# Attention on one Trainium2 core: which engine's guests stand in which PSUM bank, one down projection moved, unread products in two waits

## The reference

```python
x = x + attention_0(layernorm(x), ctx, W_k, b_k, ln_gamma, ln_beta)  # keys = values = ctx @ W_k.T + b_k
x = x + ffn_0(layernorm(x), w_gate, w_up, w_down)
x = x + attention_1(layernorm(x), ctx, ctx)                          # 32 query heads, 8 key-value heads of 16
x = x + moe(layernorm(x), gate_w, w0, w1, wo)                        # 8 experts, the best 2 of a token
```

```python
def h_bitlinear(x, w):
    return einsum('bsh,oh->bso', act_quant(fwht(x)), weight_quant(w))
y = h_bitlinear(silu(h_bitlinear(x, w_gate)) * h_bitlinear(x, w_up), w_down)
```

## Time and profile before

| | us |
|---|---|
| median of 3 runs | 1672.63 |
| lowest, highest | 1671.73, 1675.54 |
| span of the profiled execution | 1670.3 |

### The profile page before, as it was taken

The page is one execution under the profiler, slowest core; times in us unless marked ns, Lnnn a source line. Parts: engine busy times, 40 slices in busy tenths (PEclk is TensorE's granted clock), DMA queues, the critical chain, the costliest instruction groups (busy, mean ns, idle before and its releaser), DMA issues.

```text
span 1670.3 us, 24439 instructions
## 1 busy us (share of the span) xinstructions
PE 1567.2 (94%) x8124; PEld 1047.5 (63%) x8150; DVE 948.0 (57%) x1539; ACT 717.6 (43%) x1160; POOL 702.1 (42%) x479
## 2 busy tenths in 40 slices
PE   6869999999889999999899899999999999999998
PEld 4555657565543434434333778788788888788886
DVE  6998979796878897887885622222122222222221
ACT  5885646455547777777677211111111111111111
POOL 1124251633513125254354765670862180930064
PEclk9889999999898999999999999999999999999999
DMA  9189800000231445243430625231440140530088
GB/s 357 56 305 386 291 1 1 0 1 1 84 94 47 123 132 149 82 126 111 148 114 28 224 70 189 82 120 32 182 176 26 59 155 26 188 127 26 26 140 213
DMA packets 90944, 196.16 MB, mean 117 GB/s; under 512 B 7153, under 2 KB 9074, under 8 KB 90226
## 3 DMA queue, kind: packets, MB, share of 16 engines
q1 hardware_dynamic: 71746, 156.68, 28.2%
q0 software_dynamic: 7168, 17.04, 4.5%
q10 hardware_dynamic: 11952, 21.43, 3.9%
HBM read 113.28 MB, written 81.32 MB: 117 GB/s over the span
## 4 chain that ended last, share of the span: by engine, by line
PE 68%; DVE 16%; POOL 6%; ACT 4%; issue 3%; DMA 3%; another core or an unknown queue 0%; SPq 0%; POOLq 0%; DVEq 0%; ACTq 0%
PE psum L2929 11%; PE psum L2931 11%; PE psum L2930 11%; PE psum L2580 6%; DVE neg_max L2057 5%; PE psum L2782 5%; PE psum L2771 5%; PE psum L2744 4%; POOL expert_weight_parts L1052 3%; PE psum L2625 3%; PE psum L2595 2%; DMA w_of_even_expert<-in_L_ffn_w 2%; PE psum L2953 2%; POOL expert_weight_parts L1051 1%; DVE inner_rotated_t_second L1926 1%
## 5 line engine op out<-in xcount | busy, mean ns | idle before, releaser
L2057 DVE TENSOR_REDUCE neg_max<-psum 128x2 f32<-128x1024 f32 x248 | 291.3, 1220 | 49.5 <-PE psum L2744 48.3
L1420 ACT ACTIVATE probabilities<-psum 128x512 f32<-128x512 f32 x512 | 271.7, 601 | 85.2 <-PE psum L2771 81.3
L2199 DVE TENSOR_TENSOR expert_inner<-psum,expert_inner 128x512 f32<-128x512 f32 x78 | 53.9, 692 | 388.7 <-ACT expert_inner L1526 378.6
L2929 PE MATMUL psum<-expert_weight_parts,sorted_tokens_t_first 128*128 x624 | 250.8, 402 | 8.8 <-POOL expert_weight_parts L1052 5.1
L2930 PE MATMUL psum<-expert_weight_parts,sorted_tokens_t_first 128*128 x624 | 246.8, 396 | 0.0
L2931 PE MATMUL psum<-expert_weight_parts,sorted_tokens_t_second 128*128 x624 | 246.8, 395 | 0.0
L1526 ACT ACTIVATE expert_inner<-psum 128x512 f32<-128x512 f32 x78 | 46.7, 599 | 396.7 <-PE psum L2931 396.7
L2771 PE MATMUL psum<-query_rows,key_rows 50*128 50x512 f32 x512 | 179.3, 444 | 4.1 <-ACT probabilities L1420 3.0
L2744 PE MATMUL psum<-key_rows,query_rows 48*128 48x512 f32 x496 | 170.6, 491 | 11.7 <-DVE neg_max L2057 5.8
L2929 PEld LDWEIGHTS psum<-expert_weight_parts,sorted_tokens_t_first 128*128 128x128 f32 x624 | 117.7, 189 | 37.4 <-issue 11.1
L2782 PE MATMUL psum<-probabilities,value_and_one 128*32 128x512 f32 x1024 | 140.3, 620 | 0.8 <-ACT probabilities L1420 0.7
(11 more groups left out here) (316 smaller groups left out, 2924.3 us busy)
## 6 DMA issues: line engine op xcount, KB each, us to landing
sorted_x<-zero_rows SPq DMA_DIRECT2D x9, 3960.0 KB, 30.5
w_of_odd_expert<-in_L_ffn_w SPq DMA_DIRECT2D x8, 2048.0 KB
wo_of_expert<-in_L_ffn_wo SPq DMA_DIRECT2D x7, 2048.0 KB, 8.6
query_rows<-query_rows_of_units SPq DMA_DIRECT2D x64, 192.0 KB, 3.5
w_of_even_expert<-in_L_ffn_w SPq DMA_DIRECT2D x6, 2048.0 KB, 11.6
sorted_tokens<-sorted_x ACTq DMA_DIRECT2D x39, 264.0 KB, 2.8
sorted_y<-expert_out ACTq DMA_DIRECT2D x39, 256.0 KB
query_rows_of_units<-dims_first SPq DMA_DIRECT2D x32, 256.0 KB
```

The source lines that it names most:

```text
L1420: nc.scalar.activation(prob[t % 2][:, i * SEQ:(i + 1) * SEQ], bank[4 + n % 3], ACT.Exp, scale=HD ** -0.5).then_inc(c_e, 1)
L2057: nc.vector.tensor_reduce(of_pair[:, p, st, :], ring(("max", (m, i))).rearrange("p (h n) -> p h n", h=2), AX.X, ALU.max, negate=True).then ...
L2199: nc.vector.tensor_tensor(h, bank[2 * half + 1], h, ALU.mult).then_inc(e_h, 1)
L2929: nc.tensor.matmul(out_bank, hi[:, cols], w_r[:, bass.ds(w_at, 512)], start=start, stop=False)
```

## The change

- In phase C the jobs that ACT reads (`chunk`, `xt`, `logits`, `pick`, `rank`) leave the ring and take a bank of the scores' rotation over 4, 5 and 6, in ACT's own order. DVE's jobs keep the ring of two slots. `xt` is cut from two jobs of two token tiles (1024 columns) to four jobs of one (512 columns), in steps 1, 2, 3 and 3.
- From unit 30 on the scores rotate over five banks, 2 to 6, and DVE's few jobs over banks 0 and 1. The `attend` that stood between the third and the fourth score product there now comes behind the fourth.
- In the last batch of phase B, `down_projected(b - 1, 3)` leaves round 3 and stands behind the loop, its transposes in round 6 rather than 2, the copy of these, the update of x and the statistics accordingly. Behind it come three chunks, then `unread(16)`; the fourth chunk moves behind tile 1's rotation.
- `unread(24)` near the end of phase A, before `scales_spread(0)`; `unread(3)` behind each pair of maxima in unit -1.

```diff
@@ jobs and places
+        OF_VECTOR = ("router sums", "x dims")
+        jobs, jobs_at_end = [("negmax", 0)], []
...
+                of_ = jobs if there(u_ + 2) else jobs_at_end
...
+        place = {job: i % 2 for i, job in enumerate(jobs)}
+        place.update({job: 2 + i % 2 for i, job in enumerate(jobs_at_end)})
...
+        last_scores = scalar_jobs.index(("score", 16 * (UNITS - 2)))
+        scalar_place = {job: (4, 5, 6)[i % 3] for i, job in enumerate(scalar_jobs[:last_scores])}
+        scalar_place.update({job: (2, 3, 4, 5, 6)[i % 5] for i, job in enumerate(scalar_jobs[last_scores:])})
@@ ScalarE, phase B
                 silu_pair(b, 2)
-                if b:
+                if b and more:
                     inner_transposed(b - 1, 3)
...
+                else:
+                    inner_transposed(b - 1, 3)
                 silu_pair(b, PAIRS - 1)
@@ VectorE, phase B
-                    if b and r == 4:
+                    if b and more and r == 4:
                         tokens_updated(b - 1, 3)
...
                 second_part_of(b, 0, 1)
+                if not more:
+                    tokens_updated(b - 1, 3)
                 second_stage(b, 1)
...
+                if not more:
+                    tokens_statistics(b - 1, 3)
+                    queries_deviation(b - 1)
                 tokens_updated(b, 0)
@@ TensorE
                 weight_transposed(18)
+                unread(24, bank[4])
                 scales_spread(0)
...
-                    if b and r == 2:
+                    if b and r == (2 if more else 6):
                         inner_quantised_transposed(b - 1, 3)
-                    if b and r == 3:
+                    if b and more and r == 3:
                         down_projected(b - 1, 3)
...
-                    for chunk in (CTX_CHUNK, 0, 1, 2):
+                    down_projected(b - 1, 3)
+                    for chunk in (CTX_CHUNK, 0, 1):
                         chunk_transposed(0, chunk)
+                    pe.wait_ge(b_g, BATCH * FC)
+                    unread(16, bank[4])
...
                 if not more:
+                    chunk_transposed(0, 2)
                     chunk_transposed(0, 3)
...
+                of, at = (scalar_held, scalar_place[job]) if job in scalar_place else (held, place[job])
+                if at == 2 and of is held and held[2] is None:
+                    held[2] = held[3] = held[0]
+                if of is scalar_held and at == 2 and scalar_held[2] is None:
+                    scalar_held[2] = scalar_held[3] = held[1]
+                if of[at] is not None:
+                    pe.wait_ge(*of[at])
...
-                if n >= 3:
-                    pe.wait_ge(c_e, n - 2)
+                take(("score", n), c_e, n + 1)
...
-                                if p == 1 and h == 1 and not there(u + 2):
-                                    attend(ST * u + t - 1)
                                 score(u, t, p, h)
                             if there(u + 2):
                                 maximum(u + 2, 2 * t + p, 1 - h, h == 0)
+                        if u == -1:
+                            unread(3)
...
-            def batch_transposed(b, half):
-                pe.wait_ge(d_xn, b * ST + 2 * half + 2)
+            def batch_transposed(b, st):
+                pe.wait_ge(d_xn, b * ST + st + 1)
```

78 lines of the change are left out of this document (42 added, 36 removed).

## The result

The changed kernel takes 1661.8 us (median of 5 runs), the kernel before 1672.6 (5 runs): ratio 0.9934, 95% interval 0.9921 to 0.9947. The profiled execution of the changed kernel has a span of 1659.9 us, 10.4 less than before's 1670.3. My forecast was 1664.5.

A forecast was written before the change was run, and what follows sets the result against it. TensorE, busy 1567.2 of 1670.3 us, bounds the kernel; time lies in its idle, low clock or removable work. Terms 3.8 + 4.0 + 0.4 + 0.1 + 0.0 - 1.0 + 0.8 = 8.1 us gave 1662.2, plus 2.3: 1664.5 us; range 1657 to 1670.5.

The forecast's parts named there:

- The ternary gap: TensorE's idle stretch before the last batch's inner rotation: moving one down projection there and filling it saves 3.8 us.
- only about 0.3 survive: Inner rotation: of 2.6 us from a warm clock, about 0.3 us remain because VectorE is late next.
- The guests: ScalarE's jobs in attention's score banks: routing waits vanish, 1.0 us for each of three batches, 0.5 per rank, 4.0 us.
- My own steps (-0.83, +0.2, +0.3, -0.5): Routing in attention, one batch: first guest step 4.70 to 3.87 us, next +0.2, then +0.3, next unit's first step -0.5.
- The clock and the chunks: Mid attention: fewer stalls keep TensorE's clock up, 0.8 us; plain chunks in the score banks save at most 0.4 us.
- The start of attention: Unread products behind eight pairs of maxima cost 0.4 us and warm the clock: 0.1 us gained, ends -2.5 and +2.0.
- Phase A: 24 unread products before the products of the scales: 0.0 us, since TensorE waits for ScalarE anyway; ends -0.6 and +0.9.
- The last two units: End of attention: GpSimd's closed chain turns TensorE's gain into a longer VectorE wait: -1.0 us, ends -2.5 and 0.
- Rival A: End of attention: the last two units' gain carries through, +3.3 in place of -1.0, giving 1660.2 us; chance 0.12.
- D: Attention: guests take a score bank, so the next step's third product waits for their copy; slower, 1679.3 us; chance 0.07.
- C: Waits only change place: routing gives 1, the clock nothing, the ternary gap 3.45, the end -1: 1669.2 us; chance 0.15.
- B: Clock stays up at attention's start, the rotation's first tile and two of four falls: 1658.5 us; chance 0.10.

The follow-up runs named there:

- kind B: Label of chips, not a kernel: those of the first two groups of follow-up runs, where the kernel before took 1663.2 and 1663.7 us.
- the pair of kernels that differ there in nothing else: The kernel before with only ScalarE's guests moved into the score banks, ratio 0.9985, against the kernel before with the ternary part alone, ratio 0.9991.
- kind A: Label of chips, not a kernel: those of the first measurement and the last group of runs, where the kernel before took 1672.6 and 1673.6 us.
- the kernel with three banks: The changed kernel with the last two units as before the change (three score banks to the end): 1656.7 us, ratio 0.9961 to the kernel before.
- the last kernel: The changed kernel with batch 2's slots and row weights on VectorE and no unread products at all: 1659.6 us, ratio 0.9900 to the kernel before.

## Why the prediction was right, point by point

**The sum.** 8.1 us forecast, 10.4 measured. The terms were off both ways: the guests gave 2.7 more, clock and chunks 1.0 more, the last two units 0.8 more; the ternary gap and the start gave 0.5 less each, phase A with the loops behind it 0.35 less, and what comes behind the shift took 1.0. That they nearly cancel is luck, and so in part is the chip: on kind B the changed kernel gains 4.7 us (2.7 to 6.5), which 8.1 would have missed.

**The ternary gap**, 3.8 forecast, 3.3 measured. The 3.45 us of the loop came, the clock stayed up, and VectorE was late next, as worked out; the fill overran by 0.2 us instead of leaving 0.3. What failed is the step "only about 0.3 survive": nothing does, it is -0.1. Counted from the end of the loop, which was itself 0.35 late, the rotation starts 4.15 us earlier and not 3.45, because VectorE's steps ahead of it are less stretched (its first second stage takes 1.22 us for 2.17). Of that 3.8 are left at VectorE's `second_part_of` for tile 1, which comes 6.6 us behind TensorE's start and not 6.0, 3.6 at the quantising and 3.3 at the transposed maxima. I had costed the moved transposes and chunks at nothing; but GpSimd's split of the chunk behind the second tile now falls on VectorE's second stages (1.63 and 2.31 us for 1.21 and 1.22). Without the fill and with a cold start the stage is shorter: 24.66 to 24.67 us in four traces, 25.76 to 25.78 in all seven others of the place, six with the fill and one without it in which the clock stayed up. So what goes with the 1.1 us is whether the first tile runs cold, and that only the kernels without the fill did; that it then misses GpSimd's split is my reading. So the fill is not worth 0.3 us but costs up to 1.1. (Without the ternary part the stage takes 25.49, 25.45 and 24.67 us, the last with a shorter stretch at half clock: it is as sensitive there.) What I had said of the moved update of x held: 0.74 us beside GpSimd's subtraction, not stretched.

**The guests**, 4.0 forecast, 6.7 measured in these units, and 6.7 confirmed by the pair of kernels that differ there in nothing else. The mechanism was right and a term was mis-sized: a batch is worth 1.84, 1.85 and 1.5 us and not 1.0, a rank 0.75 and not 0.5. My own steps (-0.83, +0.2, +0.3, -0.5) add up to 0.83, which I wrote as 1.0. Step by step in units 12 and 13: 4.70 to 3.63 (I said 3.87), +0.16 (+0.2), +0.06 (I said +0.3), 4.60 to 3.93 (I said 0.5, it is 0.67), and the third step of unit 13, which I took as "small change", gave 0.33.

**The clock and the chunks**, 0.8 + 0.4 forecast, 2.2 between units 1 and 29 beside the routing units, 1.4 of it the fall at 628. That fall is in both traces of the kernel before and in one of the four traces of kind A with the guests; on kind B it is in no trace, without the guests either. So that the change took it away is not shown. The rest is not separable.

**The start of attention**, 0.1 forecast, -0.4 measured, within the ends. The pair with its unread products takes 1.30 us and not 1.18: I had added up the records and one start, not the step into and out of the full-row products twice per pair. The unread products did shorten the stretch at half clock: 3.4 to 13.7 us in the six traces with them, 13.7 to 23.9 in the eight without. But with them it begins at 504 to 507 us, behind the wait, and without them at 491 to 497, so that part of it passes ahead of that wait. Over all traces the start takes 34.9 to 38.4 us without the unread products and 35.6 to 39.6 with them. Warm products before a wait did not keep the clock up behind it.

**Phase A**, 0.0 forecast: nothing separable from the 0.35 us that the changed kernel lost by the start of batch 3's loop.

**The last two units**, -1.0 forecast, -0.2 measured. All of its parts but one are in the trace: the wait of 0.96 us for the last maxima (0.9 said), 2.9 us of lead that TensorE makes behind it (10.5 at unit 30, 13.4 at the last attended transposes), of which 2.1 are lost again in VectorE's wait of 2.99 us (3 us or more said) for GpSimd (0.91 before). The clock did fall over the last logits (in the changed kernel, line 2898 from 910.28 on):

```profile
909.20:912.50 3.30, 3.30 (x11) 0.75 (x10) 2.55 (x9) 0.86 (x2) 2.39 (x4) 0.50 0.78 291
```

But the 0.7 us for it did not reach the shift, which waits for GpSimd's reciprocal root. Rival A is excluded: kernels with three and with five banks end within 0.2 us.

**Rivals.** D, guests that take a score bank, is excluded by the units' lengths. C, the waits only change place, holds for the last two units alone; its total, 3.4 us, lies within what kind B shows, but not by its mechanism, for the units won 6.7 there too. B, the clock stays up, came true in the rotation, where it brought nothing, and at 628, and was false at the start and in unit 17.

**What stays open**: why a chip is of kind A or B, and with it why the gain over before is 0.66% on the one and 0.28% on the other (single traces put that difference between units 2 and 29: 8.9 us won there against 3.1); the 4 us total of the kernel with three banks; and the total of the last kernel.

## What to carry to other kernels

An engine's queue can be full of short waits that all have one cause, a shared ring; giving the guests to the ring of the engine that copies them out was worth two thirds more than counting its visible waits had said (6.7 us for 4.0). Before speeding up a stage, follow the chain of the engine that ends it last: here TensorE's faster units were worth nothing until GpSimd's small steps went to the idle VectorE, and moving GpSimd's long work beside VectorE's short steps cost more than it gave (6.3 us for 4.4). Don't pay for a warm clock with filler ahead of a wait unless a trace shows what the cold one costs: of three fillers none is shown to have earned its time.

## What the runs showed of the hardware that I had not expected

- GpSimd's cast or subtraction of 128x2048 elements holds a VectorE instruction of 128x4 or 128x32 elements with two inputs in SBUF until it is done: 1.84 us for 0.16, 4.38 for 0.19.
- An idle time of TensorE of 3.11 to 3.12 us ahead of the inner rotation was followed by a fall of its clock in four kernels (from 431 to 434 or 435 us) and by none in a fifth; the same program part, on three chips.
- Behind the scatters in units 17 and 24, ScalarE or VectorE take up finished products up to 2.5 us late on the chips of kind A, in all six traces, and on those of kind B in none of eight, with 298 and 297 GB/s of DMA in the two stretches shown. Units 22 to 26 differ by 3 to 7 us between the kinds, with falls of the clock among it.
- The same kernel on the same chip varies by 0.6% (1653.3 to 1664.0 us), with the mean granted clock (0.983 and 0.976 in these two runs) going along.
